# An expert layer whose experts finish their own rows, in place of a scatter-added sum buffer with one normalisation pass at the end

## The chip, the cores and the metric

The kernel runs on one NeuronCore of one Trainium2 chip. The time is device microseconds of one execution; a smaller one is better. The profile is one execution taken by the hardware profiler. PE is TensorE, DVE VectorE, ACT ScalarE, POOL GpSimd and SP the sync engine, which here issues the plain DMAs.

## The reference, cut to what matters

One decoder layer over x of 16 batches x 256 tokens x 256 features (4096 tokens). A state-space mixer and a cross attention come first, each followed by a residual sum and a layer norm. Then comes a mixture of 8 experts, two for each token, and the last residual sum and norm:

```python
dot2 = einsum('bsh,eh->bse', x2, expert_embeddings)    # 4096 x 8
vals, idx = top_k(dot2, 2); w = softmax(masked dot2)
# expert e takes at most CAP = 512 of its tokens
y = w * (relu(xe @ W1[e].T) @ W2[e].T)                 # 256 -> 512 -> 256
out = layernorm(x2 + sum of y over the token's experts)
```

## The kernel before, in words

All matrix products are made of three single-pass products of rounded parts (`three`, lines 611 to 613), so each operand exists as a `_hi` and a `_lo` tile: ACT rounds the one, DVE subtracts it for the other.

The first stage, `body`, goes through the 16 batches, 8 heads each, with the mixer of later batches and the routing of the batch before woven in. In head 3 POOL makes the rows of the batch before (`xrow`, line 2110) from `xb` with the mean and the reciprocal root of the variance; SP writes them to the DRAM buffer `accd` (line 561). In head 0 of the next batch POOL scatters each row to two places of the DRAM buffer `slots`, one for each of its two experts, with four indirect DMAs (line 1972). A slot is 260 columns: the row, its token number, two weights and the number of the first expert.

`ending` does the same for the last batch and also runs its 256 rows through expert 0 (`block_inner`, `block_outer`), since they come too late for expert 0's slots; the sum is `acc`, which is the buffer `xa`.

The second stage goes through experts 0 to 7. PE's order for expert e is `inner(e)` (24 products of 512 columns), `rows(e + 1)` (8 transposes of the next slots, line 834) and `outer(e)` (48 products of 256 columns, two tiles of 128 rows at a time; the first needs `h_lo` tile 0). Around it stand, in program order on each engine: on ACT `parts` (the next weights), `relu` (`h_hi`), `xparts` and `result` (`yo`, the expert's 512 output rows times their weights); on DVE `parts` (`w_lo`), `relu` (`h_lo`), `xparts` and `weights`; on SP the loads of the slots of expert e, and, between those of experts 2 and 3, ten weight loads of 512 KB (line 457) and the write of `acc` into `accd` (line 588), which waits until the scatter-adds of expert 0 are done. POOL adds `yo` into `accd` with four indirect accumulating DMAs for each expert (`add`, line 2174), and expert e's wait for all those of expert e - 1. Expert 6 runs tile by tile in the order `T_ORDER` = 0, 2, 1, 3, expert 7 in halves (`last_inner`, `last_outer`).

When all scatter-adds are done (line 600), SP reads `accd` back into `fx` in 12 pieces, 32 rows of 256 a partition. DVE takes the moments (`bn_stats`, `bn_aggr`), POOL the power -0.5 (line 2184), ACT scales (line 1378), SP writes `out` (line 603). Every engine runs its own instructions in the order of the program; only semaphores tie them together.

## Time and profile before

| | before |
|---|---|
| time, median of 3 runs (lowest to highest) | 1028.47 us (1027.39 to 1030.19) |
| span of the profiled execution | 1025.7 us |
| busy share of PE / PE weight loads | 96% / 91% |
| busy share of DVE / ACT / POOL | 79% / 71% / 55% |
| share of the chain that ended last: PE / ACT / DVE / DMA | 77% / 8% / 6% / 3% |

The profiled execution's own time is its span, 1025.7 us from its first instruction to its last, and what lies around it. Busy shares are means over the whole span; which engine bounds a stage is read from a table by stretches of time and from the chain of work that ended last. A duration in a row is that of the instruction on its engine; the time from a DMA's issue to its landing is another view.

### The profile page before, as it was taken

To read this page: it belongs to the slowest core of one execution; us is meant where nothing else is said; L and a number is where in the kernel's file an instruction comes from. 1 tells how busy PE (TensorE), PEld (TensorE's weight loads), DVE (VectorE), ACT (ScalarE), POOL (GpSimd) and SP (SyncE) were. 2 spreads that over 40 slices of the span, in tenths; PEclk is the share of its full clock that TensorE was granted. 3 is DMA by queue.
4 is the path that set the end of the run, shared out by engine and by line. 5 is a ranking of instruction groups with operands and counts; after the bars stand their busy time and mean duration, and the time that the engine had idled before them with its cause. 6 is when DMAs were issued, how large, how long until landed. Compare 5 with 4: busy or idle time off the path is not lost.

```text
span 1025.7 us, 21471 instructions
## 1 busy us (share of the span) xinstructions
PE 979.9 (96%) x7018; PEld 929.5 (91%) x7018; DVE 809.4 (79%) x2040; ACT 729.3 (71%) x1865; POOL 568.7 (55%) x967
## 2 busy tenths in 40 slices
PE   8999999999999999999999999999999999999960
PEld 7799999999999999999999999999999999899960
DVE  6887878887888888888888888878887877655526
ACT  6686868787777777776877787868786766365536
POOL 4743464656566556554656566545656463526543
PEclk9999999999999999999999999999999999999985
DMA  7643031213111311113110311041105110386448
GB/s 248 220 135 110 6 118 36 61 35 108 47 50 46 101 53 51 45 59 96 51 45 30 125 51 46 17 137 50 47 11 171 33 41 11 140 293 126 67 60 315
DMA packets 63829, 89.60 MB, mean 87 GB/s; under 512 B 14932, under 2 KB 44680, under 8 KB 63720
## 3 DMA queue, kind: packets, MB, share of 16 engines
q1 hardware_dynamic: 56040, 75.51, 22.8%
q0 software_dynamic: 7680, 12.72, 5.8%
q8 instruction: 58, 0.95, 0.4%
q14 instruction: 51, 0.42, 0.1%
HBM read 49.21 MB, written 38.99 MB: 86 GB/s over the span
## 4 chain that ended last, share of the span: by engine, by line
PE 77%; ACT 8%; DVE 6%; issue 3%; DMA 3%; POOL 1%; SPq 0%; ACTq 0%; DVEq 0%; POOLq 0%
PE ps L611 20%; PE ps L612 20%; PE ps L613 20%; PE ps L640 7%; PE ps L719 3%; DVE nmx L1800 2%; DMA accd<-yo,tku 1%; ACT fx L1378 1%; PE ps L655 1%; PE ps L757 1%; PE ps L657 1%; POOL accd L2174 1%; ACT hp L1076 1%; ACT ys_x L1179 1%; ACT prob L1237 1%
## 5 line engine op out<-in xcount | busy, mean ns | idle before, releaser
L2085 POOL TENSOR_SCALAR prob<-prob,rinv 128x333 f32<-128x333 f32 x256 | 144.4, 575 | 242.1 <-DVE rinv L1809 241.1
L1232 ACT ACTIVATE oT_hi<-ps 128x256 fp32r<-128x256 f32 x126 | 48.5, 385 | 151.4 <-PE ps L657 151.4
L611 PE MATMUL ps<-kv_lo,w_hi 128*128 128x256 f32 (+1 forms) x512 | 154.4, 302 | 1.1 <-DVE kv_lo L1386 1.1
L613 PE MATMUL ps<-kv_hi,w_hi 128*128 128x256 f32 (+1 forms) x512 | 153.4, 300 | 0.0
L612 PE MATMUL ps<-kv_hi,w_lo 128*128 128x256 f32 (+1 forms) x512 | 153.1, 299 | 0.0
L1237 ACT ACTIVATE prob<-ps,nmx 128x333 f32<-128x333 f32 x256 | 135.0, 538 | 7.4 <-DVE nmx L1800 7.4
L1386 DVE TENSOR_TENSOR pT_lo<-ps,pT_hi 128x512 fp32r<-128x512 f32 x254 | 131.8, 550 | 1.1 <-ACT pT_hi L1249 0.3
L1800 DVE TENSOR_REDUCE nmx<-ps 128x2 f32<-128x666 f32 x128 | 108.3, 846 | 9.3 <-PE ps L613 7.9
L640 PE MATMUL ps<-ident,prob 128*128 128x128 f32 (+1 forms) x768 | 105.5, 272 | 1.8 <-POOL prob L2085 1.0
L611 PEld LDWEIGHTS ps<-kv_lo,w_hi 128*128 128x128 f32 x512 | 96.9, 189 | 1.6 <-issue 1.5
L612 PEld LDWEIGHTS ps<-kv_hi,w_lo 128*128 128x128 f32 x512 | 96.5, 189 | 0.0
L613 PEld LDWEIGHTS ps<-kv_hi,w_hi 128*128 128x128 f32 x512 | 96.6, 189 | 0.0
L640 PEld LDWEIGHTS ps<-ident,prob 128*128 128x128 f32 (+1 forms) x768 | 90.1, 140 | 6.2 <-issue 1.6
L1447 DVE SCALAR_TENSOR_TENSOR cv<-hp,vec,cv 128x256 f32<-128x256 f32 x192 | 87.7, 475 | 1.8 <-ACT cv L1124 1.8
L611 PE MATMUL ps<-k_lo,q_hi 128*128 128x334 f32 x256 | 81.0, 317 | 1.9 <-DVE k_lo L1392 1.9
L1392 DVE SCALAR_TENSOR_TENSOR k_lo<-ps,vec,k_hi 128x334 fp32r<-128x334 f32 x128 | 71.6, 559 | 12.2 <-ACT k_hi L1055 11.7
L612 PE MATMUL ps<-k_hi,q_lo 128*128 128x334 f32 x256 | 81.0, 317 | 0.0
L613 PE MATMUL ps<-k_hi,q_hi 128*128 128x334 f32 x256 | 80.6, 315 | 0.0
L611 PE MATMUL ps<-w_lo,oT_hi 128*128 128x256 f32 x254 | 77.5, 305 | 0.2 <-DVE oT_lo L1386 0.2
L2174 POOL DMA_INDIRECT accd<-yo,tku x32 | 52.4, 1637 | 45.4 <-ACT yo L1322 20.0
L1249 ACT ACTIVATE pT_hi<-ps 128x512 fp32r<-128x512 f32 x127 | 77.1, 607 | 0.4
L1972 POOL DMA_INDIRECT slots<-xrow,slot_u x60 | 63.4, 1057 | 21.4 <-issue 20.3
(308 smaller groups left out, 3284.6 us busy)
## 6 DMA issues: line engine op xcount, KB each, us to landing
wraw<-in_W SPq DMA_DIRECT2D x14, 512.0 KB, 7.9
vcd_hi<-vst_hi SPq DMA_DIRECT2D x10, 512.0 KB, 2.7
vcd_lo<-vst_lo SPq DMA_DIRECT2D x10, 512.0 KB, 3.5
v_hi<-vcd_hi SPq DMA_DIRECT2D x32, 154.0 KB
v_lo<-vcd_hi SPq DMA_DIRECT2D x32, 154.0 KB
slots<-initr SPq DMA_DIRECT2D x8, 520.0 KB, 7.8
xs<-in_x SPq DMA_DIRECT2D x16, 256.0 KB, 4.4
xts<-in_xT SPq DMA_DIRECT2D x15, 256.0 KB, 4.1
```

The lines of the kernel that those rows point to most:

```text
L611: pe.matmul(dst, hi1, lo2, start=first, stop=False, skip_group_check=True)
L612: pe.matmul(dst, lo1, hi2, start=False, stop=False, skip_group_check=True)
L613: return pe.matmul(dst, hi1, hi2, start=False, stop=last, skip_group_check=True)
L640: last = pe.transpose(ps[0:r, far if j == 2 else T0, (j % 2) * S + t * P:(j % 2) * S + t * P + P], prob[:, ring, t, j * P:j * P + r], iden ...
L1237: act.activation(prob[:, h % 2, t, 0:KEYS], ps[:, S0 + t, 0:KEYS], ACT.Exp, bias=nmx[:, h % 2, t:t + 1], accum_out=rsum[:, h % 2, t:t + 1] ...
L1249: act.activation(pT_hi[:, 0:2, :].rearrange("p j s -> p (j s)"), ps[:, T0, :], ACT.Copy).then_inc(pTh_set, 1)
L1386: return dve.tensor_tensor(dst, src, ap(hi), ALU.subtract)
L1392: dve.scalar_tensor_tensor(out=k_lo[:, idx % 2, :], in0=g[:, 0:KCOL], scalar=vec[:, V_BK + idx:V_BK + idx + 1], in1=ap(k_hi[:, idx % 2, :] ...
L1447: op = dve.scalar_tensor_tensor(out=cv[:, ct, :], in0=hp[:, ct, k:k + S], scalar=w, in1=cv[:, ct, :], op0=ALU.mult, op1=ALU.add)
L1800: dve.tensor_reduce(nmx[:, h % 2, :], ps[:, S0:S0 + NT, 0:KEYS], AX.X, ALU.max, negate=True).then_inc(nmx_set, 1)
L1972: pool.indirect_dma_start(slots, bass.IndirectOffsetOnAxis(slot_u[:, 2 * t + c:2 * t + c + 1], 0), rows[:, t, :], None).then_inc(sc_done, 16)
L2085: pool.tensor_scalar(prob[:, h % 2, t, 0:KEYS], prob[:, h % 2, t, 0:KEYS], rinv[:, h % 2, t:t + 1], 1.0, ALU.mult, ALU.mult).then_inc(norm ...
```

## The change

Each expert finishes its rows. `accd`, the scatter-adds and the pass over `fx` are gone. A slot gets a 261st column, the place where the token's sum so far lies, which is its lower-numbered expert's slot; the last batch's rows lie in a new part at the head of `slots` (`OWN` rows), where SP writes `acc`. For expert e:

- POOL gathers the sums so far into `bs` with four indirect DMAs (`gather`); expert 0's are its slots themselves, one plain load.
- DVE adds `bs` to `yo` (`sums`), takes the moments (`moments`), and SP writes the sums back to the slots (`keep_sums`), two DMAs for each expert, four for expert 6. The gather of expert e + 1 waits for them.
- POOL makes the power (`power`), DVE the shift, ACT the scaled rows `fo` (`scale`), and POOL scatters them into `out` with four indirect DMAs without accumulation (`finished`). A token that two experts took is written twice, the second time with its full sum; a scatter waits for those of the expert before.
- For expert 7 DVE does the weighting, the sum and the scaling itself (`last_sums`, `last_scale`).

In the first stage POOL also makes `xo`, the row normalised twice, which SP writes to `out` for tokens that no expert takes; `xrow` is made by an add of the negated mean. DVE has two more small instructions for it in each batch, the power runs over 4 columns in place of 2. `last_places` and `last_slots` have some more small instructions, and the last batch's own rows are normalised between expert 0's steps on DVE (`block_moments`, `block_norm`). The diff, cut to its core (`variance`, `power`, `finished` and the setup are left out; they do what is said above):

```diff
-ROW = D + 4
+ROW = D + 5
+OWN = NT * P
+TRASH = OWN + E * CAP
...
-                    need(sp, x2_set, 2 * c + 2)
-                    sp.dma_start(acc_rows[bass.ds(c, 1)].rearrange("o p t d -> (o p) t d"),
-                                 rows_out(b)[:, :, 0:D]).then_inc(x2_st, 16)
+                    need(sp, xo_set, 2 * c + 2)
+                    sp.dma_start(out_rows[bass.ds(c, 1)].rearrange("o p t d -> (o p) t d"), xo[:]).then_inc(xo_st, 16)
...
-            for e in range(2, E):
-                if e == 3:
-                    sp.wait_ge(wo_mm, 8 * B)
-                    expert_weights(range(3, 4), wr_ld[1])
-                    expert_weights(range(4, E), w1r_ld)
-                    sp.wait_ge(acc_set, 2 + NT)
-                    sp.wait_ge(add_done, 64)
-                    sp.dma_start(acc_rows[B - 1], acc[:]).then_inc(x2_st, 16)
+            sp.dma_start(bs[0][:], slot_rows[0]).then_inc(bs0_ld, 16)
+            def slots_of(e):
                 sp.wait_ge(xt_mm, 2 * (e - 1))
-                sp.wait_ge(wsl_set, e - 1)
-                sp.wait_ge(tku_set, e - 1)
+                sp.wait_ge(cols_set, 3 * (e - 1))
                 sp.dma_start(xsl[e % 2][:], slot_rows[e]).then_inc(xsl_ld[e % 2], 16)
-            sp.wait_ge(add_done, 64 * E)
-            def rows_of(d, c):
-                return d[P * FO[c]:P * (FO[c] + FR[c]), :].rearrange("(p r) d -> p r d", p=P)
-            for c in range(LC):
-                sp.dma_start(fx[:, FO[c]:FO[c] + FR[c], :], rows_of(accd, c)).then_inc(part_ld[c], 16)
-            for c in range(LC):
-                sp.wait_ge(fy_set, c + 1)
-                sp.dma_start(rows_of(out, c), fx[:, FO[c]:FO[c] + FR[c], :]).then_inc(out_st, 16)
-            sp.wait_ge(out_st, 16 * LC)
+            def keep_sums(e, tiles, done):
+                sp.wait_ge(z_set, done)
+                sp.dma_start(slot_rows[e][:, tiles, 0:D], yo[e % 2][:, tiles, :]).then_inc(z_st, 16)
...
+            slots_of(2)
+            sp.wait_ge(wo_mm, 8 * B)
+            expert_weights(range(3, 4), wr_ld[1])
+            expert_weights(range(4, E), w1r_ld)
+            sp.wait_ge(acc_set, 2 + NT)
+            sp.dma_start(own_rows, acc[:]).then_inc(own_st, 16)
+            slots_of(3)
+            sp.wait_ge(acc_set, 5 + 2 * NT)
+            sp.dma_start(out_rows[B - 1], lo[:]).then_inc(last_st, 16)
+            for e in range(E - 1):
+                if e < E - 2:
+                    keep_sums(e, slice(0, 2), 2 * e + 1)
+                    keep_sums(e, slice(2, 4), 2 * e + 2)
+                else:
+                    for n, s in enumerate(T_ORDER):
+                        keep_sums(e, slice(s, s + 1), 2 * e + n + 1)
+                if e + 4 < E:
+                    slots_of(e + 4)
+            sp.wait_ge(last_st, PART + 16)
+            sp.wait_ge(xo_st, 16 * (B - 1))
+            sp.wait_ge(sc_done, 64 * B + 64 * E)
...
+                scale(e - 1, (0, 1), e - 1)
                 if e < E - 2:
-                    result(e, u)
+                    result(e, u, (0, 1))
+                    scale(e - 1, (2, 3), e - 1)
+                    result(e, u, (2, 3))
...
+            last_relu(0, (0, 1))
+            scale(E - 2, T_ORDER[0:3], E - 2)
+            last_relu(0, (2, 3))
             last_relu(1, (0, 1))
-            last_result(0)
-            last_result(1)
+            scale(E - 2, T_ORDER[3:4], E - 1)
...
+            def base_of(e, half):
+                if e == 0:
+                    dve.wait_ge(bs0_ld, PART + 16)
+                else:
+                    dve.wait_ge(bs_ld[half], 32 * e)
+            def sums(e, half):
+                u, o = e % 2, slice(2 * half, 2 * half + 2)
+                dve.wait_ge(yo_set, 4 * e + 2 * half + 2)
+                base_of(e, half)
+                dve.tensor_tensor(yo[u][:, o, :], yo[u][:, o, :], bs[u][:, o, 0:D], ALU.add).then_inc(z_set, 1)
...
+            def moments(e):
+                dve.wait_ge(z_set, 2 * e + 2)
+                for s in range(ST):
+                    last = dve.bn_stats(f_st[:, e, s, :], yo[e % 2][:, s, :])
+                last.then_inc(fstat_set, 1)
+                variance(e, e, slice(0, ST))
...
+            sums(0, 0)
             for e in range(1, E - 1):
                 u = e % 2
+                sums(e - 1, 1)
+                moments(e - 1)
+                relu(e)
+                shift(e - 1, e - 1, slice(0, ST))
+                xparts(e + 1)
                 parts(e + 1, 1 - u)
-                relu(e)
-                xparts(e + 1)
                 weights(e + 1, 1 - u, 16 * ((e + 1) // 2) + (16 if u == 0 else 0))
-            for half in range(2):
-                for i in range(I // P):
+                if e < E - 2:
+                    sums(e, 0)
...
+                for s in tiles:
+                    dve.wait_ge(o_mm, 2 * (E - 2) + s + 1)
+                    base_of(e, s // 2)
+                    dve.scalar_tensor_tensor(out=yo[u][:, s, :], in0=ps[:, Y_LAST[s], 0:D], scalar=wsl[:, e, s:s + 1],
+                                             in1=bs[u][:, s, 0:D], op0=ALU.mult, op1=ALU.add).then_inc(z_set, 1)
+                    dve.wait_ge(z_set, 2 * (E - 2) + ST + s + 1)
+                    last = dve.bn_stats(f_st[:, e, s, :], yo[u][:, s, :])
+                last.then_inc(fstat_set, 1)
+                variance(part, e, slice(tiles[0], tiles[-1] + 1))
...
+            last_sums((0, 1), E)
+            last_sums((2, 3), E + 1)
+            last_scale((0, 1), E)
+            last_scale((2, 3), E + 1)
...
-                            pool.tensor_scalar(xrow[:, t, 0:D], xb[:, t, :], c_mv[:, t, 0:1], c_rs[:, t:t + 1],
-                                               ALU.subtract, ALU.mult).then_inc(x2_set, 1)
+                            pool.tensor_scalar(xrow[:, t, 0:D], xb[:, t, :], c_nm[:, t:t + 1], c_rs[:, 0, t:t + 1],
+                                               ALU.add, ALU.mult).then_inc(x2_set, 1)
+                        need(pool, xo_st, 16 * (b - 1))
+                        for t in range(NT):
+                            pool.tensor_scalar(xo[:, t, :], xb[:, t, :], c_nm[:, t:t + 1], c_rs[:, 1, t:t + 1],
+                                               ALU.add, ALU.mult).then_inc(xo_set, 1)
...
+                pool.wait_ge(cols_set, 3 * e + 1)
                 if e == 1:
-                    pool.wait_ge(x2_st, 16 * B)
-                for n, s in enumerate(T_ORDER if e == E - 2 else range(ST)):
-                    need(pool, yo_set, 4 * e + n + 1)
-                    pool.indirect_dma_start(accd, bass.IndirectOffsetOnAxis(tku[u][:, s:s + 1], 0), yo[u][:, s, :],
-                                            None, compute_op=ALU.add).then_inc(add_done, 16)
-            add(0, 0)
-            for e in range(1, E):
-                add(e, e % 2)
-            for c in range(LC):
-                pool.wait_ge(fstat_set, 3 * c + 3)
-                pool.tensor_tensor(f_rs[:, FO[c]:FO[c] + FR[c]], f_vv[:, FO[c]:FO[c] + FR[c]], powm[:, 0:FR[c]], ALU.pow).then_inc(frs_set, 1)
+                    pool.wait_ge(own_st, PART + 16)
+                pool.wait_ge(z_st, PART + 32 * e + (32 if e == E - 1 else 0))
+                for s in range(ST):
+                    pool.indirect_dma_start(bs[e % 2][:, s, :], None, slots,
+                                            bass.IndirectOffsetOnAxis(tku[:, e, s, 1:2], 0)).then_inc(bs_ld[s // 2], 16)
...
+            for e in range(1, E - 1):
+                power(e - 1, e - 1, slice(0, ST))
+                gather(e)
+                finished(e - 1, range(ST))
+            power(E - 2, E - 2, slice(0, 3))
+            power(E - 1, E - 2, slice(3, 4))
+            finished(E - 2, (0, 1), T_ORDER)
+            gather(E - 1)
+            finished(E - 2, (2, 3), T_ORDER)
+            power(E, E - 1, slice(0, 2))
+            power(E + 1, E - 1, slice(2, 4))
+            finished(E - 1, range(ST))
```

PE's instructions and their order are the same in both. On POOL, from the scatter of the last batch's rows on (`xrow_b`), the start of the expert stage was before, with the scatter-adds of experts 0 and 1 (`add_done` is the semaphore of the scatter-adds that have landed):

```order
L1972 DMA slots<-xrow_b,slot_u 4608x260 [waits xs0_ld0,xs0_ld1,slot_set,route_step]
L1972 DMA slots<-xrow_b,slot_u 4608x260 x3
L2174 DMA accd<-yo,tku 4608x256 [waits yo_set,tku_set]
L2174 DMA accd<-yo,tku 4608x256 [waits yo_set] x3
L2174 DMA accd<-yo,tku 4608x256 [waits x2_st,yo_set,add_done,tku_set]
```

and is now, with the power of the last batch (`l_rs`) and of expert 0 (`f_rs`), the gather of the sums so far for expert 1 (`bs`) and the scatter of expert 0's finished rows (`out`); `part_ld1` and `part_ld2` are the semaphores of SP's writes of expert 0's sums and of the last batch's:

```order
L2097 DMA slots<-xrow_b,slot_u 4864x261 [waits xs0_ld0,xs0_ld1,slot_set,route_step]
L2097 DMA slots<-xrow_b,slot_u 4864x261 x3
L2332 TENSOR_TENSOR l_rs<-l_vv,powm 128x2 [waits acc_set]
L2306 TENSOR_TENSOR f_rs<-f_vv,powm 128x4 [waits fstat_set]
L2315 DMA bs<-slots,tku 128x261 [waits part_ld1,part_ld2,cols_set]
L2315 DMA bs<-slots,tku 128x261 x3
L2328 DMA out<-fo,tku 4608x256 [waits fo_set,sc_done,xo_st]
L2328 DMA out<-fo,tku 4608x256 [waits fo_set] x3
```

So four issues for each expert become eight and a power, and the gather for expert e + 1 stands ahead of the scatter for expert e.

On DVE, in the middle of the expert stage, an expert (the split weights, `h_lo`, the next rows, then the columns of the next slots) was

```order
L1386 TENSOR_TENSOR w_lo<-wraw,w_hi 128x1024 [waits wh_set] x2
L1789 SCALAR_TENSOR_TENSOR h_lo<-ps,h_hi 128x512 [waits hh_set] x4
L1386 TENSOR_TENSOR xs_lo<-ps,xs_hi 128x512 [waits xth_set] x2
L1839 CAST tku<-xsl 128x4 [waits yo_set,add_done,xsl_ld0]
L1841 SCALAR_TENSOR_TENSOR wa<-xsl,ef 128x4 [waits ef_set]
L1843 SCALAR_TENSOR_TENSOR wb<-xsl,ef 128x4
L1846 TENSOR_TENSOR wsl<-wa,wb 128x4 [waits wab_set]
L1847 TENSOR_SCALAR ef<-ef 128x1
```

and is now, its columns (not shown) last as before,

```order
L1894 TENSOR_TENSOR yo<-yo,bs 128x512 [waits bs_ld0,yo_set]
L1894 TENSOR_TENSOR yo<-yo,bs 128x512 [waits bs_ld1,yo_set]
L1918 BN_STATS f_st<-yo 128x6 [waits z_set]
L1918 BN_STATS f_st<-yo 128x6 x3
L1909 BN_AGGR f_mv<-f_st 128x2 [waits fstat_set]
L1909 BN_AGGR f_mv<-f_st 128x2 x3
L1912 TENSOR_SCALAR f_vv<-f_mv 128x4 [waits fstat_set]
L1828 SCALAR_TENSOR_TENSOR h_lo<-ps,h_hi 128x512 [waits hh_set] x4
L1925 SCALAR_TENSOR_TENSOR f_nm<-f_mv,f_rs 128x4 [waits frs_set]
L1399 TENSOR_TENSOR xs_lo<-ps,xs_hi 128x512 [waits xth_set] x2
L1399 TENSOR_TENSOR w_lo<-wraw,w_hi 128x1024 [waits wh_set] x2
```

The sums and the moments of the expert before now stand ahead of `h_lo`, for which PE waits, and the sums wait for the gather; `w_lo` has moved behind.

On SP, the row from the loads of the slots of expert 1 on was

```order
L580 DMA xsl<-slots 128x4x260 [waits slot_set,sc_done,rank_set,seen_set]
L592 DMA xsl<-slots 128x4x260 [waits tku_set,wsl_set,xt_mm]
L457 DMA wraw<-in_W 128x1024 [waits wo_mm]
L457 DMA wraw<-in_W 128x1024 x9
L588 DMA accd<-xa 128x2x256 [waits add_done,acc_set]
L592 DMA xsl<-slots 128x4x260 [waits tku_set,wsl_set,xt_mm] x5
```

and is now

```order
L583 DMA xsl<-slots 128x4x261 [waits slot_set,sc_done,rank_set,seen_set]
L584 DMA bs<-slots 128x4x261
L590 DMA xsl<-slots 128x4x261 [waits cols_set,xt_mm]
L463 DMA wraw<-in_W 128x1024 [waits wo_mm]
L463 DMA wraw<-in_W 128x1024 x9
L602 DMA slots<-xa 128x2x256 [waits acc_set]
L590 DMA xsl<-slots 128x4x261 [waits cols_set,xt_mm]
L605 DMA out<-lo 128x2x256 [waits acc_set]
L595 DMA slots<-yo 128x2x256 [waits z_set] x2
```

The last batch's sums (`slots<-xa`) and expert 0's (`slots<-yo`), for which the gather of expert 1 waits, are issued behind the ten weight loads, as the write into `accd` was.

## Rows read from the trace of the kernel before

**Rows 1.** Stretch; busy us of PE, PEld, DVE, ACT, POOL; clock, DMA share, GB/s.

```profile
960.00:980.00 20.00, 20.00 (x142) 18.48 (x141) 11.58 (x25) 10.40 (x20) 11.28 (x8) 1.00 0.39 42
```

**Rows 2.** The chain that ended last, its end: start, us, what.

```profile
991.95 1.55 POOL accd L2174
...
993.80 3.84 DMA accd<-yo,tku
...
1007.28 13.37 ACT fx L1378 x27
```

**Rows 3.** The last writes: timeline of SP, and their time to landing.

```profile
1019.20 2.31 SPq L603 DMA_DIRECT2D out<-fx  x4
...
out<-fx SPq DMA_DIRECT2D x2, 128.0 KB, 2.1
```

**Rows 4.** Timeline: write of `acc`, expert 2's first `outer` product, experts 5, 6.

```profile
919.71 0.38 SPq L588 DMA_DIRECT2D accd<-xa  x1
...
926.16 0.36 PE L611 MATMUL ps<-w_lo,h_hi 128*128 128x256 f32 x1
...
968.40 0.84 ACT L1322 ACTIVATE yo<-ps,wsl 128x256 f32<-128x256 f32 x2 [1.91 <-PE ps L613]
...
970.22 2.36 DVE L1386 TENSOR_TENSOR w_lo<-wraw,w_hi 128x1024 fp32r<-128x1024 f32 x2 [4.33 <-ACT w_hi L1145]
...
970.61 2.26 POOL L2174 DMA_INDIRECT accd<-yo,tku  x1 [0.30 <-issue]
...
972.50 1.88 DVE L1789 SCALAR_TENSOR_TENSOR h_lo<-ps,h_hi 128x512 fp32r<-128x512 f32 x3
...
974.60 0.37 PE L611 MATMUL ps<-w_lo,h_hi 128*128 128x256 f32 x1
...
975.24 1.28 DVE L1386 TENSOR_TENSOR xs_lo<-ps,xs_hi 128x512 fp32r<-128x512 f32 x2
...
980.58 0.47 ACT L1331 ACTIVATE yo<-ps,wsl 128x256 f32<-128x256 f32 x1 [0.95 <-PE ps L613]
```

**Rows 5.** POOL's groups by shape: count, then busy us, mean ns, idle before.

```profile
L2110 POOL TENSOR_SCALAR xrow<-xb,c_mv,c_rs 128x256 f32<-128x256 f32 x30 | 39.2, 1306 | 3.1 <-POOL c_rs L2105 2.9
...
L2105 POOL TENSOR_TENSOR c_rs<-c_vv,powm 128x2 f32<-128x2 f32 x15 | 10.9, 724 | 0.0
...
L2184 POOL TENSOR_TENSOR f_rs<-f_vv,powm 128x4 f32<-128x4 f32 x6 | 6.0, 1008 | 6.8 <-DVE f_vv L1953 6.8
```

**Rows 6.** POOL's indirect issues: count, minimum, median, maximum in ns, first to last.

```profile
L1972 POOL DMA_INDIRECT slots<-xrow,slot_u x57: 956/971/1258, 149.9 to 879.0; - x57
L2174 POOL DMA_INDIRECT accd<-yo,tku x32: 1550/1552/2418, 905.8 to 993.8; - x32
```

**Rows 7.** DMA issues: KB each, median us to landing (first: issued 905 to 906).

```profile
wraw<-in_W SPq DMA_DIRECT2D x2, 512.0 KB, 15.5
...
accd<-xa SPq DMA_DIRECT2D x1, 256.0 KB, 2.4
...
slots<-xrow_b,slot_u POOLq DMA_INDIRECT x4, 2.7
```

**Rows 8.** DMA rate while the weights load: columns of rows 1.

```profile
904.00:906.00 2.00, 2.00 (x20) 2.00 (x19) 1.68 (x3) 1.59 (x5) 0.25 (x1) 1.00 0.99 395
```

**Rows 9.** Timeline of DVE in the last pass: four tiles of 256 columns.

```profile
1007.71 1.40 DVE L1939 BATCH_NORM_STATS2 f_st<-fx 128x6 f32<-128x256 f32 x4
...
1009.14 0.38 DVE L1950 BATCH_NORM_AGGREGATE f_mv<-f_st 128x2 f32<-128x6 f32 x4
```

**Rows 10.** Granted clock behind PE's last product: columns of rows 1.

```profile
991.00:992.00 1.00, 0.76 (x7) 0.56 (x5) 0.00 (x0) 0.60 (x2) 0.23 (x2) 1.00 0.59 38
...
993.00:994.00 1.00, 0.00 (x0) 0.00 (x0) 0.00 (x0) 0.00 (x0) 0.70 (x2) 0.91 0.04 9
```

**Rows 11.** Head 4 of one batch: POOL's timeline; the chain, PE's transposes of `prob`.

```profile
543.76 1.28 POOL L2085 TENSOR_SCALAR prob<-prob,rinv 128x333 f32<-128x333 f32 x2 [0.62 <-DVE rinv L1809]
...
550.98 0.66 PE ps L640 x6
```

More of the change, by code:

```diff
@@ new lines, in variance @@
+            def variance(part, e, tiles):
+                dve.wait_ge(fstat_set, 3 * part + 1)
+                for s in range(ST)[tiles]:
+                    last = dve.bn_aggr(f_mv[:, e, s, :], f_st[:, e, s, :])
+                last.then_inc(fstat_set, 1)
+                dve.wait_ge(fstat_set, 3 * part + 2)
+                dve.tensor_scalar(f_vv[:, e, tiles], f_mv[:, e, tiles, 1], EPS, None, ALU.add).then_inc(fstat_set, 1)
+            def moments(e):
[4 more added lines that the diff above has]
+                variance(e, e, slice(0, ST))
@@ L1849, in block_weights, with block_norm @@
+            def block_norm():
+                dve.wait_ge(lrs_set, 1)
+                for t in range(NT):
+                    dve.tensor_scalar(lo[:, t, :], acc[:, t, :], l_mv[:, t, 0:1], l_rs[:, t:t + 1],
+                                      ALU.subtract, ALU.mult).then_inc(acc_set, 1)
             def block_weights():
@@ L1914, in _ @@
             relu(0)
+            block_moments()
             part1(1, 1)
@@ L2160, in body @@
                         need(pool, route_step, r + 7)
+                        for t in range(NT):
+                            pool.tensor_scalar(xrow[:, t, D + 1:D + 2], slot_a[:, t, 0:1], slot_a[:, t, 1:2], None, ALU.min)
                         pool.tensor_copy(slot_u[:], slot_a[:].rearrange("p t c -> p (t c)")).then_inc(slot_set, 1)
```

335 lines of the change are left out of this document (196 added, 139 removed).

## The prediction, as it was made before the changed kernel ran

> **What bounds the kernel now.** I read the table by stretches first. PE is busy for all 20.00 us from 960 to 980 while DVE has 11.58, ACT 10.40 and POOL 11.28 [rows 1], and PE has 96% of the span. So up to the last product, at about 991.8 (PE is busy 0.76 of the microsecond from 991, [rows 10]), the time is PE's, and another engine counts only when it makes PE wait. An expert is 24 products of 0.23 us, the transposes (0.87) and 48 products of 0.115 us, 12.05 us in all. The chain that ended last shows what stands behind PE [rows 2]: the scatter-adds issued at 991.95 and 993.80, 3.84 us to land, the read-back of the sums, 13.37 us of scaling on ACT; then the last writes, issued until 1021.5, landing in 2.1 [rows 3]. The span ends at 1025.7, some 2.4 us behind that landing: a tail of 34 us. The median, 1028.47, is 2.8 us above the span, and I add that again at the end.
>
> **The tail, removed and replaced (-17.5).** Times here are those of before. DVE has finished `xs_lo` at 976.5; `w_lo` (2.36) and the columns (0.7) keep it until 979.6 [rows 4]. Expert 6's first three tiles then cost 0.87 each (sum 0.36, wait 0.1, statistics 0.41 as 11.6 us / 32 shows in [rows 9], 1.40 for four and pipelined), and the variance 0.55: 982.9. POOL's power takes 1.0 [rows 5]: 983.9. ACT scales until 986.8. An issue of a scatter without accumulation takes 0.971 [rows 6] and 0.30 lies between issues (the idle time in the row at 970.61, [rows 4]), so 1.27 each, and it lands 2.7 after its start [rows 7]. POOL cannot scatter expert 6's rows before expert 5's have landed. Expert 5's `yo` is ready at 969.24 [rows 4], its sums at 970.6, their write lands at 974.2, the gather for expert 6 is issued to 979.3, the last scatter of expert 5 at 983.1: landed at 986.0 with a wait. Then come two scatters and the gather for expert 7, issued from 988.6, the last at 992.4, landed at 995.2. `last_sums` of two tiles with their moments takes 2.7: 998.0. Power (0.72, [rows 5]) and the first scaling: 999.3. Four issues: the last at 1003.1, landing at 1005.8. With the 2.4 us behind a landing the span would end at 1008.2, that is -17.5. The late `h_lo` tiles on DVE make PE pause about 2 us near 985, which this chain through POOL does not feel. Ends: 6 us less if POOL waits for nothing at 986, 3 us more if the gather takes 0.6 more for each issue.
>
> The Trainium skill, *DMA: Bandwidth & Descriptors*, "Anatomy of one DMA — SWDGE (gpsimd) path", puts a fixed 2 us and the bytes at the engines' full rate for such a DMA; as an estimate that is 2.3 us for 134 KB. The trace has 2.7 for the scatter, which stands above in the sum; by the page the tail would be some 0.8 us shorter, with two landings in it.
>
> **The last batch's routing and rows (+1.4).** The power over 4 columns in place of 2 costs 1.01 against 0.72 [rows 5], so +0.3; two small DVE instructions and those that `last_places` and `last_slots` gain, at 0.15 to 0.2 each, push expert 0's steps: +0.6, together +0.9. `block_moments` (1.3) and `block_norm` (0.75) stand ahead of `xs_lo` for expert 1; DVE had some idle time there, and I take +0.5 of the 2.05, bounds 0 and 2.
>
> **The stall at expert 2's `outer` (+7.0).** This is the term of which I am least sure. Before, the sums of the last batch were written at 919.71 behind the ten weight loads, waiting for scatter-adds, and landed in 2.4 us [rows 4, 7]; nothing on PE waited for them. Now the gather for expert 1 waits for them and for expert 0's sums, the sums of expert 1 on DVE wait for the gather, and `h_lo` of expert 2 stands behind the sums. SP's queue is loaded with 5.24 MB of weights (a load issued at 905 took 15.5 us, [rows 7]), four slot loads of 0.53 MB with the new one for `bs`, and 1 MB of writes: 8.4 MB, at the 395 GB/s that the stretch shows [rows 8] 21 us from about 901.8, so 922.8, and 1.5 for the last landing: 924.3. The fourth gather is issued 3.8 later and lands in 2.8: 930.9. The sum of two tiles takes 0.65 (`xs_lo`, as wide, is 1.28 for two, [rows 4]), the moments 2.1 (1.40, 0.38, 0.17 and the waits between, [rows 9]), `h_lo` 0.69: about 934.6. PE wants its first `outer` product at 926.16 [rows 4] plus the 1.4 above, 927.6. That is 7.0 us. It is 9.5 if the gathered rows take 0.6 us more an issue, 5 if the loads reach 440 GB/s.
>
> **The clock behind the stall (+1.8).** When PE ran dry at 991.8, the granted clock was still 0.91 from 993 to 994 [rows 10] and 0.50 after that. A pause of 7 us would end at 0.50, and PE's products then run at 1.2 GHz until the clock is back. No row of this kernel shows the way up behind a pause. Nothing to 5.6 us (all of one `outer`) are the ends; the way down is the nearest row, about 2 us, and I take 1.8.
>
> **Experts 2 to 6 (0).** From the last sum to the next one the loop is: write of the sums 2.4 to 3.5 (2.4 for the same size in [rows 7]), four issues 3.8 and a landing 2.8, sum 0.65, that is 10 to 11.5 us, and PE's 12.05 cover it. POOL has a power (1.0, wait 0.2) and eight issues of 1.27: 11.4 us, under 12.05. DVE puts 2.75 ahead of `h_lo`, whose first tile stood at 972.50 with `yo` ready at 969.24; now 972.9, and PE wanted it at 974.60 [rows 4]. `w_lo` ends at about 979 and is wanted near 980.2. ACT's four scaling passes (2 us) go into its idle time. If POOL's cover of 0.65 is gone, each expert costs what is over.
>
> The pause that is nearest here is an issue beside DVE. At 970.61 one took 2.26 us, beside `w_lo` from 970.22 [rows 4], against a median of 1.552 [rows 6]: 0.7 more for one of four. If it comes once an expert, POOL's cycle is 12.1 and just at the bound, worth nothing or a few tenths.
>
> **The body (0).** POOL makes `xo` besides `xrow`, two more of 1.31 us [rows 5] a batch, and the power is 0.3 longer: up to 2.9 us late for head 4's `prob`. One such pair is ready at 545.1 and PE transposes it at 550.98 [rows 11], so 5.9 us cover it. That cover also hides DVE's two small instructions.
>
> **Sum.** -17.5 + 0.9 + 0.5 + 7.0 + 1.8 = -7.3, so a span of 1018.4 and, with 2.8, a time of 1021.2 us.
>
> **The rivals.** (a) No stall: the loads get through sooner, or the writes overtake the weights on other engines. For it: the write at 919.71 landed in 2.4 us [rows 7]. Then the 8.8 us of stall and clock go: 1012.4. (b) The gather is as slow as the accumulation, 1.552 + 0.30, since it too reads DRAM rows by an index [rows 6]. POOL's cycle is 13.7, 1.65 over PE's: four experts 6.5, less the 3.2 that the stall at expert 2 had already given, and 2.3 in the tail: +5.6, 1026.8. Against it: the plain scatter of 260 columns takes 0.971. (c) The slower one: POOL's queue becomes the bound because all eight issues cost 1.85, through the indices of 261 columns or contention with DVE. The cycle is 16.0, 3.95 over; over four experts 15.8 less 3.2, and twelve issues of the tail at 0.58 more are 7.0: +19.6, 1040.8. It decides from a mean of about 1.57 us an issue, where its loss eats the gain; the bound itself begins at 1.36. For it speaks the row of 2.26. The Trainium skill, *SBUF — State Buffer*, "Who interferes with whom", says that a VectorE instruction with two SBUF inputs contends with GpSimd's reads, while writing descriptors takes the other interface (which it calls inferred); by that, (c) through contention would get next to nothing, 1021.2 staying as it is. The row at 970.61 lies beside just such an instruction and is longer, so I leave (c) its share. (d) The change does something else in the body: `xo` delays `prob`, and with it PE in 15 batches. It needs the 5.9 us of cover to be gone; at the 2.3 us of `xo` it would be up to 35 us, 1056.
>
> **How the numbers follow.** The forecast has 52%, (a) 20%, (b) 14%, (c) 9%, (d) 5%. The forecast's own range, with its ends for stall, clock and tail, is 1015 to 1028. The range of 8 in 10 goes over (a), down to 1010.5 with the shorter tail, and over (b), up to 1031 with its clock term at the upper end; (c) and (d) are left out. A measurement can tell 0.3%, 3.1 us, from no change: 1025.4 to 1031.6. Faster: all of (a) and the forecast but its last tenth or so, 0.71 with a little of (b); same: most of (b), 0.15; slower: (c) and (d), 0.14.
>
> **What would show it.** Right: a pause of PE ahead of `outer` of expert 2, between about 927 and 935, with DVE's sum waiting for `bs`, and a clock of 0.50 behind it; indirect issues for `bs` and `out` of about 0.97 us; elsewhere no pauses but 2 us near 985; 16 to 17 us from PE's last product to the end; a first stage as long as before. Wrong: no pause there (a), a pause at each expert with POOL busy throughout (b, c), or a first stage longer by over 2 us (d). I would be most wrong if the sums' write waits for something in SP's queue that the rows of before don't show.

## The result: slower by 0.4%

| | before | after |
|---|---|---|
| time, median of 6 runs each | 1027.93 us | 1032.08 us (1030.90 to 1033.86) |
| ratio to before, 95% interval | | 1.0041 (1.0029 to 1.0053) |
| span of the profiled execution | 1025.7 us | 1030.1 us |
| PE's last product to the end of the span | 33.9 us | 14.2 us |
| busy share of PE / DVE / ACT / POOL | 96 / 79 / 71 / 55% | 96 / 80 / 70 / 57% |

The forecast was 1021.2 with a range to 1031.0; the result lies 1.1 us above the range, and on the other side of no change. The tail did shrink, by 19.7 us. But PE's last product came 24.1 us later.

The waits of PE show where (engine, line, what it waited for, us in total, times, longest). The first row is of the start of the kernel, the others of the stretch from 870 us on:

```profile
PE ps L727 <- DMA xts<-in_xT: 3.1, 1, 3.1
```

```profile
PE ps L625 <- DVE h_lo L1828: 11.7, 3, 9.6
PE ps L625 <- DVE h_lo L2044: 3.0, 2, 1.7
```

The chain that ended last goes, from 914 us on, through the loop that the change brought in. Its DMAs and two of SP's rows in it (start, us, what; the other rows of the chain stand between them):

```profile
914.86 6.73 SPq L605
921.64 2.20 SPq L595
923.88 7.77 DMA slots<-yo
...
936.34 2.69 DMA bs<-slots,tku
...
947.78 4.63 DMA bs<-slots,tku
...
961.18 4.52 DMA bs<-slots,tku
...
974.46 4.67 DMA bs<-slots,tku
...
1004.68 2.66 DMA out<-fo,tku
...
1016.37 2.78 DMA bs<-slots,tku
```

By PE's own marks, which are the same instructions in both traces, the loss adds up as follows (starts in PE's timeline, but for the last row).

| where PE stands | before | after | lost there |
|---|---|---|---|
| products `xpw` of the last batch | 804.45 | 809.21 | 4.8 |
| transposes of expert 3's slots | 925.37 | 931.95 | 1.8 |
| transposes of expert 4's slots | 937.44 | 955.27 | 11.2 |
| transposes of expert 7's slots | 973.80 | 994.09 | 2.5 |
| last product ends | 991.8 | 1015.9 | 3.8 |

The sum is 24.1; less 19.7 in the tail it leaves the 4.4 between the spans. Of the last 3.8, PE's two waits for the last expert's `h_lo` are 3.0.

**The first 4.8 us** are at the very start, where the prediction had no term at all. PE's products `xpw`, which start at 58.13 and 112.61 us in the kernel before, are 0.25 us later and then 5.1 us later in the changed one. SP clears its DRAM buffers there with ten DMAs, all in `slots`, in place of nine, eight in `slots` and one in `accd`. The load of `xts`, which SP issues behind them, lands (KB and us, before and then after):

```profile
xts<-in_xT SPq DMA_DIRECT2D x1, 256.0 KB, 8.0
```

```profile
xts<-in_xT SPq DMA_DIRECT2D x1, 256.0 KB, 12.9
```

In the kernel before, PE doesn't wait for it. The timeline of PE in the changed kernel, and the table by stretches (columns as in [rows 1]):

```profile
67.50 2.96 PE L727 MATMUL ps<-xts,inw 128*128 128x256 f32 x8 [3.08 <-DMA xts<-in_xT]
```

```profile
66.00:72.00 6.00, 4.50 (x18) 3.99 (x19) 1.25 (x3) 1.68 (x5) 2.61 (x2) 0.72 0.33 84
```

The wait is 3.1 us, and the granted clock of 0.72 behind it takes about 1.7 more. From there to the last batch the distance stays between 5.1 and 4.8 us.

**The 11.2 us** are the predicted stall, and more. SP's timeline:

```profile
906.08 0.36 SPq L583 DMA_DIRECT2D xsl<-slots  x1
906.48 0.51 SPq L584 DMA_DIRECT2D bs<-slots  x1
907.09 0.45 SPq L590 DMA_DIRECT2D xsl<-slots  x1
907.58 5.25 SPq L463 DMA_DIRECT2D wraw<-in_W  x10
912.88 1.10 SPq L602 DMA_DIRECT2D slots<-xa  x1
914.44 0.38 SPq L590 DMA_DIRECT2D xsl<-slots  x1
914.86 6.73 SPq L605 DMA_DIRECT2D out<-lo  x1
921.64 2.85 SPq L595 DMA_DIRECT2D slots<-yo  x2
```

POOL's gather for expert 1 waits for the last of these, DVE for the gather, PE for DVE (start, us, and in brackets the idle time and what ended it):

```profile
932.47 1.05 POOL L2315 DMA_INDIRECT bs<-slots,tku  x1 [13.63 <-DMA slots<-yo]
```

```profile
936.73 0.69 DVE L1894 TENSOR_TENSOR yo<-yo,bs 128x512 f32<-128x512 f32 x1 [11.54 <-DMA bs<-slots,tku]
939.12 0.69 DVE L1894 TENSOR_TENSOR yo<-yo,bs 128x512 f32<-128x512 f32 x1 [1.70 <-DMA bs<-slots,tku]
```

```profile
942.61 0.55 PE L625 MATMUL ps<-w_lo,h_hi 128*128 128x256 f32 x1 [9.63 <-DVE h_lo L1828]
```

Behind the wait PE runs at 1.2 GHz until about 945.3, its products 0.21 us apart in place of 0.12, which is the rest of the 11.2:

```profile
943.00:946.00 3.00, 3.00 (x17) 3.00 (x17) 3.00 (x7) 1.09 (x2) 2.49 (x3) 0.58 0.28 83
946.00:950.00 4.00, 4.00 (x35) 3.95 (x34) 2.75 (x6) 1.88 (x5) 3.10 (x3) 1.00 0.39 83
```

**The later experts** lose 2.5 us, with PE waiting at experts 4 and 5 (0.81 and 1.26 us), since a turn of the loop takes longer than the 12.1 us that PE needs for an expert. DVE's second sum has the gather ahead of it each time:

```profile
952.50 0.69 DVE L1894 TENSOR_TENSOR yo<-yo,bs 128x512 f32<-128x512 f32 x1 [3.72 <-DMA bs<-slots,tku]
...
965.79 0.69 DVE L1894 TENSOR_TENSOR yo<-yo,bs 128x512 f32<-128x512 f32 x1 [3.59 <-DMA bs<-slots,tku]
...
979.22 0.69 DVE L1894 TENSOR_TENSOR yo<-yo,bs 128x512 f32<-128x512 f32 x1 [3.76 <-DMA bs<-slots,tku]
...
990.88 0.69 DVE L1894 TENSOR_TENSOR yo<-yo,bs 128x512 f32<-128x512 f32 x1 [1.98 <-DMA bs<-slots,tku]
```

The first three are 13.3 and 13.4 us apart, the last 11.7. The landings in the chain say why: 4.5 to 4.7 us for the first three. The fourth's last gather was issued at 987.90 and its sum starts at 990.88, 3.0 later. Beside the first three SP had issued a load of slots (rows of SP at 948.25, 961.65 and 974.93); for the fourth there is none left to load.

The rest of a turn is longer than it looks too. The gather stands behind `power` in POOL's order, `power` needs the moments of the same sums, and it ended 0.1 to 1.1 us after the write of those sums had landed (for expert 4: written at 966.51, landed in 2.5; `power` until 969.67, the gather at 969.87). So from the start of the second sum to the first gather 4.1 to 4.6 us pass.

**The issues themselves** were as forecast: POOL's 28 gathers have a median of 0.97 us, as the plain scatters of [rows 6], not the 1.552 of the accumulating ones (count, then minimum, median and maximum in ns, then the first and the last start in us):

```profile
L2315 POOL DMA_INDIRECT bs<-slots,tku x28: 946/972/1674, 932.5 to 1016.4; - x28
```

### The profile page after: what moved, and what is told of

The parts are those of the page before. It is cut to its first block, busy times and chain, and to the rows that moved or that the text cites. A ratio compares the mean times of both kernels' runs of the same rounds, so it can differ in the third digit from the quotient of the medians.

```text
span 1030.1 us, 21649 instructions
## 1 busy us (share of the span) xinstructions
PE 984.8 (96%) x7018; PEld 930.8 (90%) x7018; DVE 823.0 (80%) x2087; ACT 725.6 (70%) x1857; POOL 587.0 (57%) x1069
## 3 DMA queue, kind: packets, MB, share of 16 engines
q1 hardware_dynamic: 57496, 71.90, 22.5%
## 4 chain that ended last, share of the span: by engine, by line
PE 70%; DVE 7%; ACT 7%; DMA 5%; issue 5%; POOL 4%; SPq 2%; POOLq 0%; DVEq 0%; ACTq 0%
PE ps L625 18%; PE ps L627 18%; PE ps L626 18%; PE ps L654 7%; PE ps L733 2%; DMA bs<-slots,tku 2%; POOL bs L2315 2%; DVE nmx L1839 1%; PE ps L771 1%; PE ps L669 1%; DMA xts<-in_xT 1%; PE ps L671 1%; POOL out L2328 1%; ACT hp L1090 1%; SPq L526 1%
## 5 line engine op out<-in xcount | busy, mean ns | idle before, releaser
L1405 DVE SCALAR_TENSOR_TENSOR k_lo<-ps,vec,k_hi 128x334 fp32r<-128x334 f32 x128 | 71.6, 559 | 12.1 <-ACT k_hi L1069 11.5
L1413 DVE SCALAR_TENSOR_TENSOR q_lo<-ps,vec,q_hi 128x256 fp32r<-128x256 f32 x128 | 55.8, 477 | 24.3 <-ACT q_hi L1077 24.2
```

The lines of the kernel that those rows point to most:

```text
L1405: dve.scalar_tensor_tensor(out=k_lo[:, idx % 2, :], in0=g[:, 0:KCOL], scalar=vec[:, V_BK + idx:V_BK + idx + 1], in1=ap(k_hi[:, idx % 2, :] ...
```

## Experiments

All of them compute the whole layer. Times are medians beside runs of the kernel before on the same chip, whose median was 1027.1 to 1027.9 us; ratios are to that kernel, with 95% intervals, and can differ a little from the ratio of the medians. The changed kernel is 1.0041, 1032.1 us. The name in brackets is that of the run.

**The row of a slot, 264 columns** (`pad264`). A row of 261 is 1044 bytes, which 16 does not divide; the 1040 bytes of before are a multiple of 16, and so are 1056. The edit (the unused columns are set to zero once):

```diff
-ROW = D + 5
+ROW = D + 8
```

> The slots' row is padded from 261 to 264 columns, 1056 bytes in place of 1044; nothing else changes. Theory A, the pitch of 1044 bytes slows the clears: they land in about 8 us again (median, 9.9 in the changed kernel), PE doesn't wait for xts near 64 us, and the time falls by 4 to 5 us, to about 1027.5. Theory B, it is the tenth and eleventh issue with their bytes: no change in the first stage, 1032. What the pitch does to gathers and to the writes of the sums would show as a shorter loop for each expert.

1027.7 us, ratio 1.0006 (0.9996 to 1.0015): 4.4 us less by the medians, 3.6 by the ratios. The clears land in 7.1 us (median), `xts` in 7.4, PE doesn't wait for it, and the `xpw` products of the last batch stand at 805.14, against 804.45 before and 809.21 in the changed kernel. There are ten clears as in the changed kernel, so their number alone costs nothing here. Theory A.

**The kernel before with one column more** (`before261`).

```diff
-ROW = D + 4
+ROW = D + 5
```

> The kernel before with one unused column more in a slot (261 in place of 260), nine clears as before. Theory A (pitch): the clears' median landing rises from 7.8 to about 9.5 us, PE waits for xts near 62 us, the time rises by 3 to 5 us, to about 1032. Theory B (number of clears): within 1 us of the kernel before, 1028.

1030.3 us, ratio 1.0029 (1.0019 to 1.0039): an unused column costs 3 us in a kernel that has none of the change. PE waits for `xts` again (1.1 us). The clears are nine as before, and from 52 to 58 us the DMA engines moved 272 GB/s (last number), where the same row of the kernel before has 300, and in the 3 us behind it 215 in place of 322:

```profile
52.00:58.00 6.00, 5.78 (x42) 5.23 (x41) 5.81 (x14) 5.04 (x14) 2.40 (x4) 1.00 1.11 272
```

Only a part of it is located. The `xpw` products of the last batch stand at 809.00, 4.6 us later than before. Of that 2.1 are there at 58 us, 1.4 come between 58 and 113 us, where PE waits for `xts`, and 1.1 in small steps over the batches behind, for which no run has a cause. The first part is no sign of the row: the other profiled executions stand 0.3 to 2.3 us late at 58 us, with 1056 bytes too (1.7 in `combo6`).

**A row of 262 columns**, 1048 bytes (`pad262`).

```diff
-ROW = D + 5
+ROW = D + 6
```

> Row of 262 columns, 1048 bytes, a multiple of 8 but not of 16 as 1040 and 1056 are. If only multiples of 16 bytes or more are written at the full rate: clears at 200 to 270 GB/s near 52 to 61 us as with 1044 bytes, 1031 to 1032. If the odd number of 4-byte words is what costs: 300 to 340 GB/s as with 1056 bytes, and 1028.

1033.4 us (two runs), ratio 1.0057 (1.0036 to 1.0077). It is as slow as 261, so the odd number of words is not it. The same stretch of the clears, 52 to 58 us (the last number is GB/s), in the kernels with rows of 1044, 1048 and 1056 bytes:

```profile
52.00:58.00 6.00, 5.78 (x46) 5.70 (x46) 5.58 (x12) 5.33 (x16) 1.33 (x3) 1.00 1.07 266
```

```profile
52.00:58.00 6.00, 5.81 (x42) 5.29 (x41) 5.81 (x13) 4.86 (x14) 2.58 (x4) 1.00 1.10 280
```

```profile
52.00:58.00 6.00, 5.78 (x46) 5.47 (x44) 5.74 (x13) 5.33 (x16) 1.34 (x3) 1.00 1.09 339
```

The DMA engines are full in all three (the column before, 1.07 to 1.10), at different rates. The landings say the same (the last column is how much more than in the kernel before PE lost between its marks at 58 and 113 us):

| bytes of a row | run | clears of `slots` land in, median | `xts` lands in | PE loses |
|---|---|---|---|---|
| 1040 | before | 7.8 us | 8.0 us | |
| 1056 | `pad264` | 7.1 | 7.4 | 0.0 |
| 1044 | changed kernel | 9.9 | 12.9 | 4.9 |
| 1044 | `before261` | 8.9 | 12.3 | 1.4 |
| 1048 | `pad262` | 9.0 | 11.7 | 2.0 |

What PE loses depends on more than the row: an execution that stands 2 us late at 58 us waits less for the same landing. In the other changed kernels with 261 columns the wait for `xts` is 1.4 to 2.9 us. Four row lengths fit "a multiple of 16 bytes" (1040, 1056) against not (1044, 1048). Whether 16 is the step, or 32 with 1040 as a half case, was not tried.

**The write of `lo` behind the sums** (`lo_late`). Its issue held SP for 6.73 us.

```diff
-            sp.wait_ge(acc_set, 5 + 2 * NT)
-            sp.dma_start(out_rows[B - 1], lo[:]).then_inc(last_st, 16)
...
                     keep_sums(e, slice(2, 4), 2 * e + 2)
+                    if e == 0:
+                        sp.wait_ge(acc_set, 5 + 2 * NT)
+                        sp.dma_start(out_rows[B - 1], lo[:]).then_inc(last_st, 16)
```

> The write of the last batch's finished rows (out<-lo, whose issue took 6.73 us on SP) is moved behind the two writes of expert 0's sums. Theory A, that issue holds SP's queue: the sums are written 5 to 6 us sooner, the gather for expert 1 starts near 926 in place of 932.5, PE's wait of 9.6 us ahead of expert 2's outer falls to about 4, and the time to about 1026. Theory B, it is the bytes of the weights ahead: the next write takes the blocked issue over, the gather starts within 1 us of 932, and the time stays at 1031 to 1032.

One run only, so without an interval: 1034.5 us, no gain. The long issue moves to the sums' write, and the gather starts at 932.06 in place of 932.47:

```profile
916.01 5.91 SPq L595
921.96 9.27 DMA slots<-yo
```

So the long issue belongs to the place behind the ten weight loads, and whichever DMA comes there takes it over. Theory B. With six of the ten loads moved away (the next run) the same write of `lo` is issued in 0.66 us.

**The weights of experts 5 to 7 late** (`w_late`). 3.1 MB leave the queue ahead of the sums; ACT's waits for the weights follow (not shown).

```diff
-            expert_weights(range(4, E), w1r_ld)
+            expert_weights(range(4, 5), wr_ld[1])
...
+                if e < 3:
+                    expert_weights(range(e + 5, e + 6), (w2r_ld, w1r_ld, wr_ld[0])[e])
```

> Only the weights of experts 3 and 4 stay ahead of the sums on SP's queue; those of experts 5, 6 and 7 are issued one by one behind the sums of experts 0, 1 and 2. Theory A, the sums of expert 0 land late because 3.1 MB more of weights lie ahead of them (at about 400 GB/s 8 us): the gather for expert 1 starts near 921 to 924 in place of 932.5, PE does not wait, or under 2 us, ahead of expert 2's outer, its clock stays at 2.4 GHz there, and the time falls by 9 to 11 us from 1032.1, to 1021 to 1023. Theory B, the weights beside the gathers take back what is won: landings of 5 us and more for the gathers, and no more than 4 us gained.

1027.2 us, ratio 0.9995 (0.9979 to 1.0010): 4.9 us less, where 9 to 11 were expected. The first half is as theory A has it: the gather for expert 1 starts at 924.29, 8.2 us sooner (3.1 MB at 385 GB/s), and the wait of 9.6 us is down to 2.1:

```profile
924.29 1.05 POOL L2317 DMA_INDIRECT bs<-slots,tku  x1 [6.02 <-DMA slots<-yo]
```

```profile
934.55 0.36 PE L627 MATMUL ps<-w_lo,h_hi 128*128 128x256 f32 x1 [2.10 <-DVE h_lo L1830]
```

The gain is then given back in part, 0.7 to 1.7 us an expert: the transposes of the slots lie at 931.42, 945.89, 959.63, 972.43 and 986.26, 12.8 to 14.5 us apart (the 14.5 has the 2.1 in it). Once the stall is out, the loop of sum, write and gather is what PE waits for at each expert: DVE's second sums start at 931.06, 944.78, 957.56 and 971.34, and each waited for its gather last. In the changed kernel the stall had hidden that: PE and the loop both started anew behind it. Theory B's landings of 5 us and more are not there: from the issue of the last gather to the last three of these sums 3.8 to 4.9 us pass, in the changed kernel 4.6 to 4.8. At the last expert's transposes the kernel is 7.8 us ahead of the changed one, and 5.4 at the end.

**The slot loads behind other sums** (`slots_late`). Each is issued a sum later, so that it doesn't run beside the last gather.

```diff
-                if e + 4 < E:
-                    slots_of(e + 4)
+                if 1 <= e and e + 3 < E:
+                    slots_of(e + 3)
```

> The load of a later expert's slots is issued behind the writes of the sums of expert e - 3 in place of e - 4, so that it no longer runs beside the last gather. Theory A, that load makes the fourth gather land in 4.6 us where 2.9 are seen without it: landings of 2.9 to 3.3 us, an expert takes 12.05 to 12.4 us in place of 13.3, no PE waits at experts 4 and 5, and 3 to 4 us less, about 1028.5. Theory B, the scatters of the expert before, issued right behind, are what the gather shares the engines with: landings stay at 4.6 and the time at 1032.

1030.8 us, ratio 1.0033 (1.0023 to 1.0043). The transposes are 12.1 to 12.2 us apart (956.58, 968.75, 980.89), and of PE's three waits for `h_lo` in experts 1 to 6 one is left:

```profile
PE ps L625 <- DVE h_lo L1828: 9.4, 1, 9.4
```

DVE waits 7.9 us in all for gathers between 940 and 1000, not 13.0, and from the issue of the last gather to the sum 3.0 to 3.1 us pass where that wait is the last, not 4.6. The mechanism is A's. The time gained is 1.3 us by the medians, nearer the 2.1 us that those waits were than the 3 to 4 that I expected, and as the intervals overlap (1.0029 to 1.0053 for the changed kernel) it is not clear of the noise.

**DVE's `h_lo` ahead of the sums** (`relu_first`).

```diff
-            sums(0, 0)
...
-                sums(e - 1, 1)
-                moments(e - 1)
                 relu(e)
-                shift(e - 1, e - 1, slice(0, ST))
+                sums(e - 1, 0)
+                sums(e - 1, 1)
+                moments(e - 1)
                 xparts(e + 1)
+                shift(e - 1, e - 1, slice(0, ST))
```

> On DVE the sums and moments of expert e - 1 stand behind h_lo of expert e, and xs_lo of the next expert behind them; SP's order is that of the changed kernel. Theory A, PE's waits are DVE's queue: sums that wait for the gather hold h_lo. Expert 2's first outer then starts at once, PE has 6.5 us of other work (outer of expert 2, less the xs_lo behind the sums) before it waits, so a wait of 9.6 us becomes about 3 to 4, and the small waits at experts 4 and 5 go: 1032.1 less 8, 1024. Theory B, the loop of sum, write, gather is the bound whatever stands where: the wait moves to the next expert in full, and the time stays within 2 us of 1032.

1039.2 us, ratio 1.0106 (1.0089 to 1.0123): 7 us more, and neither theory had that. The wait at `outer` of expert 2 is gone, but PE waits 5.1 us at the next `inner` and 1.4 to 1.7 at three later ones. ACT's scaling stands ahead of its results, and waits for the moments, which now come after `h_lo`:

```profile
942.93 1.09 ACT L1353 ACTIVATE fo<-yo,f_nm,f_rs 128x256 f32<-128x256 f32 x2 [7.70 <-issue]
```

Behind it stand the result, the next weights and `h_hi`, and DVE's `h_lo` waits for that. DVE's shift, made at 942.73, is what ended this wait. By these orders a ring closes through DVE, POOL and ACT; PE's `inner` starts at 962.01, 976.15 and 990.30, so it takes 14.1 us an expert. Behind the 5.1 us PE's granted clock was 0.50 as well.

**Three edits together** (`combo3`): row of 264, late weights, late slot loads.

> Row of 264 columns, weights of experts 5 to 7 late, slot loads behind the sums of the expert three before. If the three causes are separate, their gains add: 1032.1 - 4.4 - 1.3 less 9 to 11 is 1015.5 to 1017.5. If they share one (the loop), less is gained: 1018 to 1022.

1027.3 us, ratio 0.9997 (0.9986 to 1.0007): of the 10.6 us that the three gave apart, 4.8. ACT stands still behind the scaling, ahead of a result, four times, 2.5 to 6.5 us. Two of these:

```profile
943.01 0.84 ACT L1338 ACTIVATE yo<-ps,wsl 128x256 f32<-128x256 f32 x2 [5.43 <-remote]
...
972.99 0.84 ACT L1338 ACTIVATE yo<-ps,wsl 128x256 f32<-128x256 f32 x2 [6.49 <-remote]
```

PE had ended the last product that the first of these reads at 937.5; the profile gives no releaser ("remote"). The trace is of the slowest of the ten runs, 1030.7 us.

There is a second loss, and the trace of each kernel with both the row of 264 and the late weights has it, but for `combo4`, where PE has no wait at that place: PE's clock at `outer` of expert 2. In `w_late` PE waited 2.1 us there and the granted clock stayed at 1.00; here it waited 2.0 us and the clock was 0.71 from 930 to 932 and 0.50 from 932 to 934. In the kernel with these two edits alone (`combo2`, below) the wait was 2.1, the clock 0.84, 0.50 and 0.81 in the three stretches of 2 us from 930 on, and from the transposes of expert 3 to those of expert 4 it took 16.0 us, against 14.5 in `w_late`.

**The same with `h_lo` first** (`combo4`).

> As the one before, with h_lo ahead of the sums on DVE as well. Where no PE wait is left in experts 1 to 6, this order gains only what h_lo is late (nothing to 1 us), and the later sums of the last experts push the chain that ends last by 0 to 3 us: 1015 to 1019. If the stall was still there in part, it is lower by up to 4 us.

1030.3 us, ratio 1.0020 (1.0010 to 1.0031). The ring is there from expert 1 on: PE's transposes are 14.0 to 14.1 us apart.

**Two edits** (`combo2`): row of 264 and late weights.

> Row of 264 columns and the weights of experts 5 to 7 late; the slot loads stand where the changed kernel has them. If the two gains add: 1032.1 - 4.4 - 4.9 = 1022.8, and ACT has none of the waits of 2.5 to 6.5 us behind the scaling that the kernel with all three edits showed. If those waits come from the late weights with the shorter row time, not from the slot loads: 1026 to 1028 as with three edits.

1024.0 us (1022.3 to 1032.4), ratio 0.9985 (0.9956 to 1.0014). The medians add to within 1.2 us, but two of the seven runs took 1029 and 1032, and so the interval holds 1. ACT's wait without a releaser is there once ahead of a result, 4.9 us.

**The same with the columns ahead of `w_lo`** on DVE (`combo5`).

```diff
-                parts(e + 1, 1 - u)
                 weights(e + 1, 1 - u, 16 * ((e + 1) // 2) + (16 if u == 0 else 0))
+                parts(e + 1, 1 - u)
```

> As the one before, and DVE does the columns of the next slots ahead of w_lo, so that SP's load of the next slots is issued 2.3 us sooner and runs beside the first gathers of an expert, not the fourth. Theory A, the landing of the last gather (4.6 us beside that load, 2.9 without) sets the loop: an expert takes 0.5 to 1.3 us less, 2 to 5 us in all, 1018 to 1021. Theory B, the load delays whichever gather, since all share the engines: within 1 us of the kernel without it.

1023.0 us (1019.8 to 1027.1), ratio 0.9948 (0.9930 to 0.9965). It is the first that is faster than the kernel before. Against the kernel without the edit it is 1 us by the medians and 3.8 by the ratios, whose intervals overlap, so it doesn't decide between the theories. The traces don't help: the profiled execution, at 1027.1 us the slowest of the five, has 17.9 us of ACT's waits ahead of a result in it, the one of the kernel without the edit 4.9.

**And ACT's scaling in one piece** (`combo6`), ahead of the first result; expert 6's tiles in the same way (not shown).

```diff
-                scale(e - 1, (0, 1), e - 1)
-                if e < E - 2:
-                    result(e, u, (0, 1))
-                    scale(e - 1, (2, 3), e - 1)
-                    result(e, u, (2, 3))
+                scale(e - 1, (0, 1, 2, 3), e - 1)
+                if e < E - 2:
+                    result(e, u)
```

> As the one before, and ACT scales all four tiles of the expert before ahead of its first result, where it waits for PE anyway, in place of two of them between the halves of the result. Theory A, the waits of 2.5 to 6.5 us that ACT has between the scaling and the second half of the result come from that order: they go, and the time is 1017 to 1020. Theory B, they come from something that has nothing to do with that order (a semaphore or an instruction that arrives late): they stand ahead of another instruction of ACT, and the time stays at 1022 to 1024.

1020.7 us (1017.9 to 1022.0), ratio 0.9930 (0.9916 to 0.9943): 7 us faster than the kernel before and 11 faster than the changed one. No wait of ACT is without a releaser in this trace, as theory A has it, but the time is at the edge of what A gave, the interval overlaps with that of `combo5`, and one trace is little for waits that differ from execution to execution. The order alone doesn't bring them either: the changed kernel, `pad264` and `slots_late` have it and none of these waits. What they wait for stays open: the second half of the result waits for PE's products, the stored sums of two experts before and the columns, and all three had been there.

## The prediction, point by point

- **What failed**, by size. The term of the first stage was put at nothing, with the clears of the slots in no term: 4.8 us. The stall at expert 2 was sized at 7.0 and was 9.6. The loop of experts 2 to 6 was put at nothing: 2.5 us. And PE's pauses ahead of the last expert's `h_lo` were let cost nothing: 3.0. The reading of the tail, of POOL's issues and of the place of the stall held.
- **The tail: right in size, in part by luck.** The sign that I had named, 16 to 17 us from PE's last product to the end, didn't come; it left out the pause of PE near 985 that stands in the same text. With that pause my sum gives 14.4 us (1008.2 less 993.8), and it was 14.2. But within it two errors cancel: the gather for expert 7 had landed 3.3 us after PE's end, where I had 1.4, and from the start of the last scatter to the end of the span it took 3.5 us, where I had 5.1. PE's two pauses were 3.0 us in place of 2. I let them cost nothing, since the chain through POOL did not feel them; but POOL too had been held up by the experts before, and PE's end and the chain moved together.
- **Routing and own rows, +1.4: right**, 1.8.
- **The stall at expert 2, +7.0: right place and chain, too small.** It was 9.6. PE asked for the product at 932.98, which is my 927.6 with the 4.8 us of the start and 0.6. The gather started at 932.47, 3.4 us later than my 924.3 with the same shift: I had given the sums 22.5 us from the first load, and they took 26. I had counted 8.4 MB; from 908 to 932 us alone the engines moved 8.9, at 401 to 410 GB/s between 912 and 924 but at 271 in the last 4 us. `w_late` shows that it is bytes ahead of them and `lo_late` that it is not the one long issue.
- **The clock, +1.8: right**, 1.6; the products between 942.6 and 945.3 ran at 1.2 GHz. No row of before showed the way up, so the agreement of the number is luck.
- **Experts 2 to 6, nothing: wrong, 2.5 us.** The failed step is the landing of a gather, which I took as 2.8 us, near that of a scatter that was alone [rows 7]. Beside SP's load of slots it is 4.6. The loop that I put at 10 to 11.5 us is 13.3, and 11.7 even where no load is beside it, since the gather waits for `power` behind the moments and not only for the write. The slack that I had compared it with was there, some 12.1 us (the terms that I gave for an expert add up to 11.9, not 12.05), and it was not enough. POOL was not the bound: its issues took 0.97 us and 0.30 between them, and rivals (b) and (c), by which that would be 1.85, fall. A gather ahead of `power` was not tried.
- **The body, nothing: right for `xo`, and the first stage was 4.8 us longer all the same.** This is the largest failed step. Rival (d) had a longer first stage as its sign, but named the wrong part. The clears of the slots stood in no term: I had left the setup out. The price of the 261st column was not in its bytes (0.4% more) but in the row length, as `pad264` shows, with more bytes and faster clears. With this one term the forecast would have been 1026.0; with it and the sizes of the stall and of the loop, 1031.1.
- **Issues beside DVE's `w_lo`** were longer again: the row at 972.48 took 1.67 us beside a `w_lo` from 972.11 to 974.46, against 0.98 for its neighbours. It was one issue in an expert, 0.2 to 0.7 us longer, and POOL had that to spare. The Trainium skill, *SBUF — State Buffer*, "Who interferes with whom", has such an instruction contend with GpSimd's reads but lets descriptor writing run free of it (as inferred). The trace disagrees with the second for issues that read their indices from SBUF.
- **The landing.** The Trainium skill, *DMA: Bandwidth & Descriptors*, "Anatomy of one DMA — SWDGE (gpsimd) path", gave an estimate of 2.3 us. The gathers without a load beside them took 2.7 to 3.0, so the row I had used was the better one.

## What to carry to other kernels

When a layout of a DRAM buffer changes by a few bytes, look at the row length before the number of bytes: here one unused column cost 3 us, and the part of it that was located lies at the clears of the buffer, far from the code that needed the column. When a result goes through DRAM to come back an expert later, the loop of write, gather and sum is a bound of its own: price its landings beside the loads that run at the same time, not alone. And when a small transfer is put on a path that an engine waits for, count what is queued ahead of it on its queue, and take that away first.

## What the runs showed of the hardware

- Writes of rows into DRAM with all DMA engines full: 266 GB/s with rows of 1044 bytes, 280 with 1048 and 339 with 1056, in the same 6 us of the kernel. Before, with 1040, it was 300. In the next 3 us it was 201, 240, 303 and 322 in the same order.
- A gather of 128 rows by an index costs POOL 0.97 us to issue, as a plain scatter does; the accumulating scatter took 1.55. Landing: 2.7 to 3.0 us alone, 4.5 to 4.7 beside a load of 522 KB.
- SP's issue of one 256 KB write took 6.73 us behind ten weight loads of 512 KB (`lo_late`: 5.91 for another at that place), 0.66 behind four, and 0.38 for the write of [rows 4].
- After 9.6 us without work PE ran for 2.7 us at 1.2 GHz, and after 3.1 us without work at the start of the kernel it ran slow too, the mean granted clock 0.72 over the 6 us from 66. After 1.1 and 1.4 us at that place (`before261`, `w_late`) it stayed at 1.00. After 2.1 us ahead of `outer` of expert 2 it stayed at 1.00 in `w_late` and fell to 0.50 in `combo2`.
